# Placing the turned activations and reordering five stretches of a hand-scheduled Mamba-2 and ternary-FFN layer

## The reference

```python
# block 1: Mamba-2, then a gated MLP; rmsnorm before each
h = rmsnorm(x, ln1_w)
z, xs, B, C, dt = split(h @ w_in.T)            # 512, 128, 128, 512, 4 columns
xs, B, C = silu(causal_conv4([xs, B, C]))
dt = softplus(dt + dt_bias); a = dt * -exp(A_log)
# per chunk of 128 tokens and head: cs = cumsum(a)
Y  = ((C @ B.T) * tril(exp(cs_q - cs_k))) @ (xs * dt)
Y += exp(cs) * (C @ S);  S = exp(cs[-1]) * S + sum(exp(cs[-1] - cs) * B * xs * dt)
h = x + ((Y + D * xs) * silu(z)) @ w_out.T
m = silu(rmsnorm(h, ln2_w) @ gate_w.T) * (rmsnorm(h, ln2_w) @ up_w.T)   # 1792 wide
x = layernorm(x + h + m @ down_w.T)
# block 2: weights rounded to -1, 0, 1 times their mean magnitude (q)
x = layernorm(x + ((x @ q(w_gate).T) * (x @ q(w_up).T)) @ q(w_down).T)  # 1376 wide
```

## Time and profile before

| | before |
|---|---|
| median of 3 runs | 480.82 us (480.57 to 481.75) |
| the profiled execution | 480.79 us |
| its span, first to last instruction | 478.9 us |
| PE busy | 463.3 us (97%), 2068 matmuls and transposes |
| DVE, ACT, POOL busy | 336.8 (70%), 259.7 (54%), 233.3 (49%) |
| chain that ended last | PE 85%, DVE 5%, ACT 5%, issue 2%, POOL 2% |
| mean granted clock of TensorE | 0.999 |
| DMA | 40.81 MB, 85 GB/s |

### The profile page before, as it was taken

The page is one execution under the profiler, slowest core; times in us unless marked ns, Lnnn a source line. Parts: engine busy times, 40 slices in busy tenths (PEclk is TensorE's granted clock), DMA queues, the critical chain, the costliest instruction groups (busy, mean ns, idle before and its releaser), DMA issues.

```text
span 478.9 us, 6373 instructions
## 1 busy us (share of the span) xinstructions
PE 463.3 (97%) x2068; PEld 369.1 (77%) x2068; DVE 336.8 (70%) x579; ACT 259.7 (54%) x508; POOL 233.3 (49%) x285
## 2 busy tenths in 40 slices
PE   7999999999999969999999999999999999999995
PEld 7887777876777748888878888888887777788883
DVE  3673876655587677676799899984877665587274
ACT  4889857777656656655423344222708665658000
POOL 6474555527553468767877300026028455652022
PEclk9999999999999999999999999999999999999999
DMA  7720222021222314525313336620200010000022
GB/s 239 247 88 4 86 89 66 22 89 47 75 79 91 129 42 156 184 87 192 119 58 132 133 108 205 214 90 0 85 4 0 0 46 24 1 0 1 0 89 88
DMA packets 14432, 40.81 MB, mean 85 GB/s; under 512 B 2368, under 2 KB 2368, under 8 KB 14400
## 3 DMA queue, kind: packets, MB, share of 16 engines
q1 hardware_dynamic: 14400, 40.41, 25.2%
HBM read 38.30 MB, written 2.10 MB: 84 GB/s over the span
## 4 chain that ended last, share of the span: by engine, by line
PE 85%; DVE 5%; ACT 5%; issue 2%; POOL 2%; POOLq 0%; DVEq 0%
PE psA L1712 7%; PE psA L1714 7%; PE psA L1727 4%; PE psA L1729 4%; PE psA L1718 3%; PE psA L1720 3%; PE psB L1923 3%; PE psB L1919 3%; PE psB L1922 3%; PE psA L1700 2%; PE psA L1705 2%; PE psA L1701 2%; PE psB L2010 2%; PE psB L2011 2%; PE psB L2022 2%
## 5 line engine op out<-in xcount | busy, mean ns | idle before, releaser
L796 POOL TENSOR_SCALAR var<-mv 128x1 f32<-128x1 f32 x16 | 4.5, 280 | 108.0 <-DVE mv L1293 107.9
L858 POOL TENSOR_TENSOR beta<-wsum,beta 128x512 fp32r<-128x512 f32 x28 | 36.2, 1312 | 24.5 <-ACT beta L1060 24.5
L1182 ACT ACTIVATE c<-c 128x512 f32<-128x512 f32 x14 | 8.9, 633 | 46.9 <-DVE c L1519 46.9
L1700 PE MATMUL psA<-xT_h,win_h 128*128 128x512 f32 x80 | 32.5, 407 | 0.0
L1701 PE MATMUL psA<-xT_l,win_h 128*128 128x512 f32 x80 | 31.4, 393 | 0.0
L1419 DVE SCALAR_TENSOR_TENSOR xbc<-psA,convw_sb,xbc 128x511 f32<-128x511 f32 (+2 forms) x36 | 26.9, 747 | 4.4 <-ACT xbc L1119 3.6
L1192 ACT ACTIVATE act_hl<-act 128x512 fp32r<-128x512 f32 x28 | 16.9, 627 | 17.1 <-PE psB L1923 10.9
L1712 PE MATMUL psA<-xT_h,beta 128*128 128x512 f32 x56 | 22.4, 401 | 1.0 <-issue 0.7
L984 POOL TENSOR_TENSOR int_l<-int,int_h 128x512 fp32r<-128x512 f32 x11 | 14.3, 1298 | 18.1 <-ACT int_h L1263 18.1
L1714 PE MATMUL psA<-xT_l,beta 128*128 128x512 f32 x56 | 21.9, 391 | 0.0
L1705 PE MATMUL psA<-xT_h,win_l 128*128 128x512 f32 x80 | 21.9, 395 | 0.0
(11 more groups left out here) (336 smaller groups left out, 1591.5 us busy)
## 6 DMA issues: line engine op xcount, KB each, us to landing
raw<-in_f_gu_t SPq DMA_DIRECT2D x22, 512.0 KB, 3.4
raw<-in_w_gu_t SPq DMA_DIRECT2D x14, 512.0 KB, 3.7
raw<-in_f_dn_t SPq DMA_DIRECT2D x10, 512.0 KB, 3.4
raw<-in_w_gu_t SPq DMA_DIRECT2D x14, 256.0 KB, 2.9
raw<-in_w_dn_t SPq DMA_DIRECT2D x7, 512.0 KB, 3.9
raw<-in_w_in_t SPq DMA_DIRECT2D x5, 512.0 KB, 4.0
x<-in_hidden SPq DMA_DIRECT2D x8, 256.0 KB, 5.1
out<-x SPq DMA_DIRECT2D x8, 256.0 KB, 2.0
```

The costliest lines, as they stand in the source:

```text
L858: nc.gpsimd.tensor_tensor(beta[:, f % 2, 1, cols], wsum[:, f % 2, cols], beta[:, f % 2, 0, cols].bitcast(F32), ALU.subtract).then_inc(gb_l ...
L1700: nc.tensor.matmul(ps, sh, mh, start=i == 0, stop=False)
```

## The change

Five edits; instructions are neither added nor taken away but for one ACT table load that goes and one that comes, and one wait on POOL.

1. **Placement.** A tile of 32 floats, `to_line_of_256`, is put behind x, and `FILL` grows from 8 to 40. xT_h now begins at 17664, xT_l at 34048, raw at 50432, ident at 62720, all multiples of 256; the shared region begins at 69632, a multiple of 256 as before.
2. **Batch 1's dt.** `dt 1` moves behind the last in-projection of batch 0, `dtturn 1` and `dtlog 1` move behind `inproj 1 0`, `state 0 0` and `chunk 0 1`, next to `dtend 1`. The banks of psB are dealt out anew: outproj 0 0 now reopens the bank of cb of chunk (0,1) instead of xb's, which dtturn 1 takes.
3. **Batch 1's first chunk.** The load of the MLP weights ga 2 and its splits (ACT L1040, DVE L1348) come one in-projection later, behind turn2 0 3 instead of before decay 1 0.
4. **The scan's end** (the step s = 9). `gsplit 0 0` comes first, `trest 2` before `thigh 3`, `tlow 3` directly behind it, and the copies of p1 10 and p2 8 and `gsplit 0 1` after it.
5. **The FFN's start.** ACT does `t3high` before the copies of fb 2, fa 4 and fb 3 (a new step `fbcopy` stands for two of them), `t3low` of 2 and 3 moves from POOL to DVE, and POOL waits for all four `t4low` before the weight sums of block 3.

```diff
-FILL = 8
+FILL = 40
...
-        if j == NX + NZ - 2:
+        if j == NX + NZ - 1:
             steps.append(("dt", 1))
-        if j == NX + NZ - 1:
-            steps += [("dtturn", 1), ("dtlog", 1)]
...
         if j == 0:
-            steps.append(("dtend", 1))
+            steps += [("dtturn", 1), ("dtlog", 1), ("dtend", 1)]
...
-        if j >= NX + NZ - 4 and j < NX + NZ - 1:
-            steps.append(load("ga", j - (NX + NZ - 4)))
+        if j >= NX + NZ - 4 and j != NX + NZ - 2:
+            steps.append(load("ga", min(j - (NX + NZ - 4), 2)))
...
         elif s == NX + NZ - 1:
-            steps += before + first + after + second + [("p1", NPRE - 1)] + thigh + held + [("gsplit", 0, 0)]
+            steps += first + [("gsplit", 0, 0)] + before + after + held[:1] + thigh + held[1:] + [("tlow", *turned)]
+            steps += second + [("p1", NPRE - 1), ("gsplit", 0, 1)]
...
         x = sb("x", [P, NT, D])
+        sb("to_line_of_256", [P, 32])
...
+                if f == SUM_SLOTS:
+                    pool.wait_ge(t4_low, NC)
...
-                elif kind == "t3low":
+                elif kind == "t3low" and at[0] < 2:
...
-                elif kind == "fb":
+                elif kind == "fbcopy" or kind == "fb" and at[0] not in (2, 3):
...
+                elif kind == "t3low" and at[0] >= 2:
+                    c = at[0]
+                    v.wait_ge(t3_high, c + 1)
+                    nc.vector.tensor_tensor(xT_l[:, 0:2, chunk(NC + c)], t34[:, c, 0],
+                                            xT_h[:, 0:2, chunk(NC + c)].bitcast(F32), ALU.subtract).then_inc(t3_low, 1)
```

More of the change, by code:

```diff
@@ L167, in build_schedule @@
             steps.append(load("gb", 0))
-    steps += [("tlow", NC - 1), ("t34", NC - 1), ("trest", NC - 1), ("tlast", NC - 1), ("a22", 0), ("gsplit", 0, 1),
-              ("p2", NPRE - 2), load("gb", 1), ("a22", 1), ("p2", NPRE - 1)]
+    steps += [("t34", NC - 1), ("p2", NPRE - 2), ("trest", NC - 1), ("tlast", NC - 1), ("a22", 0), load("gb", 1),
+              ("a22", 1), ("p2", NPRE - 1)]
     assert not later and NPRE == NX + NZ + 1
@@ L252, in build_schedule @@
               ("fb", 0), ("fa", 2), ("thigh3", 2), ("fb", 1), ("turn3", 3), ("t3", 2), ("t4", 2), ("tlow3", 2),
[4 rows of a table removed]
[4 rows of a table added]
     steps += [("t4high", c) for c in range(NC)] + [("t4low", c) for c in range(NC)] + [("b22low", 3)]
-    steps += [("fopen", 1), ("fb", 4), ("f7", 0), ("wide1", ALF)]
+    steps += [("fb", 4), ("f7", 0), ("wide1", ALF)]
     assert ALF == 5 and not early
```

## The result

The changed kernel takes 478.89 us as the median of 10 runs (476.43 to 479.37), the kernel before 480.88 (480.50 to 481.75); the ratio is 0.9945, with a 95% interval of 0.9933 to 0.9957. The forecast was 476.8. The ten runs stand in two groups: four from 476.43 to 477.32, all with a mean granted clock of 0.999, and six from 478.82 to 479.37, with 0.993 to 0.995. The times of the kernel before show no such gap, but its executions are not all alike either: of the 17 beside the first experiments, eight have a mean clock of 0.999 (median 480.73) and six one of 0.992 or 0.993 (median 481.50). A clock that falls after the new wait, to which it gave a chance of 0.05, happened in six of ten runs, by their mean clocks and by the one of them that was profiled.

A forecast was written before the change was run, and what follows sets the result against it. PE was taken as the bound, with little waiting left to win. The parts, -3.5 + 3.3 - 1.2 - 1.1 - 1.5 = -4.0 against 480.79, gave 476.8 us, range 473.5 to 480.2.

The forecast's parts named there:

- the new wait: At outproj (0,0), PE waits about 3.4 us until the decay operations free the bank of cb (0,1).
- Part 1: Products moving xT: aligning xT to 256 bytes saves 5.8 ns on each of 612 matmuls, -3.5 us.
- rival (a): Products moving xT: offset does nothing, the 5.8 ns belong to SBUF part or operand row length; 480.3 us, chance 0.15.
- The formula that I quoted from the Trainium skill: Warm matmuls start N/2.4 GHz plus about 2.5 ns apart, 215.7 ns for 512 columns; placement then worth 0.
- Part 2: Batch 1's dt: the late chain delays decay (0,1) and the bank outproj (0,0) reopens, +3.3 us.
- rival (d): At outproj (0,0): PE's 3.3 us wait drops the clock to 1.2 GHz; slower, 482.8 us, chance 0.05.
- My twelve microseconds at the lower level: After the wait at outproj (0,0): twelve microseconds at 1.2 GHz, each costing 0.5 us, give 482.8 us.
- Part 4: Scan's end: the new order of splits and low parts shortens PE's waits, -1.1 us, bounds 0 and -3.8.
- The bound of -3.8: Scan's end: the most that could be gained, if DVE and POOL did not stretch each other.
- Parts 3 and 5: Batch 1's first chunk without the ga 2 split, -1.2 us; FFN's start without the wait for POOL's xT_l, -1.5 us.
- rival (c): FFN's start: DVE and POOL stretch each other and nothing is won; 478.3 us, chance 0.1.
- Rival (b): Batch 1's dt: the chain costs nothing, as DVE reaches decay before PE reaches outproj or the bank differs; 473.5 us, chance 0.2.

The follow-up runs named there:

- both at 128: The kernel before with FILL 40 and no tile behind x, so xT and the shared region both lie at 128 modulo 256: 478.29 us.
- the placement alone: The kernel before with only FILL 40 and the tile of 32 floats behind x: 478.48 us, ratio 0.9944.
- dt later still: The changed kernel with dtturn, dtlog and dtend of batch 1 moved one in-projection later, behind outproj (0,0): 475.88 us.
- dt at its old place: The changed kernel with the steps of batch 1's dt where they stood before the change: 473.27 us, ratio 0.9841.
- the dt move alone: The kernel before with only the move of batch 1's dt: six runs, 484.34 to 484.37 and 486.34 to 488.17 us, ratio 1.0101.
- the region at 128: The changed kernel with FILL at 8, so xT stays at 0 modulo 256 and the shared region goes to 128: 481.48 us.

## Why the prediction was right, and where not

| part | forecast | medians | traces, from the first transposes |
|---|---|---|---|
| 1 placement | -3.5 | -2.5 | -2.7 |
| 2 dt | +3.3 | +3.4, and 2.4 more in the second group | +3.8, and 1.2 more when the clock falls |
| 3 first chunk | -1.2 | -1.0 | -0.9 |
| 4 scan's end | -1.1 | -2.7 | -2.0 |
| 5 FFN's start | -1.5 | -1.3 | -1.7 |
| sum | -4.0 | -4.1 in the first group, -2.0 over all ten | -3.5 with the clock up, -2.4 with the fall |

**Part 1** had the right size per matmul and a wrong reason and a wrong count. 5.8 ns were (4 x 8.2 + 2 x 1.5)/6 = 6.0 by the table of starts. The reason in the text was xT's own offset; rival (a) put it on the part of SBUF. Neither is so: both at 128 is as fast as both at 0. The count was too high in the FFN. From f7 0 to the last matmul the kernel with the placement alone gained 0.36 us (100.26 against 100.62) and not 1.0. The matmuls themselves did come closer there (those that move xT_h against `w` from 237 to 231 ns, where no start is delayed), but in the first blocks PE does not run at its own pace: the first product of xT against `wsums` starts at 389.06, 395.66, 402.25 and 408.84 in the kernel before and at 387.21, 393.80, 400.38 and 406.96 with the placement alone, 6.6 us apart in both. What the pitch gave is taken back by two longer distances in each block (274 to 289 ns, at most 273 in the kernel before); what paces PE there was not tried. The formula that I quoted from the Trainium skill, which gives it for an isolated matmul, has no term for the place and so gave 0 for this part; the run of the placement alone gained 2.5.

**Part 2** had the right chain. Counted from the first transposes, which start 0.86 later than in the kernel before, ecs ended at 58.45 as I took it, log at 60.07 for 60.2, dtend at 61.40 for 61.45 and decay at 62.63 for 62.8; PE was there at 59.67 for 59.45, and waited 3.1 for 3.4. Two things were not in its sum. The chunk (0,0) that "no longer stands behind dt" did not start earlier in any useful way, because it then waited 1.2 for silu; I had costed its early start at nothing, and the hole that is left there is one of the two losses in "dt later still". And the **rival (d)** was under-priced. I put its chance at 0.05 on the ground that the clock's row never fell at the two waits before. But the longer of these stands at the start, where that row doesn't show the lower level at which PE then runs (thirty transposes 0.21 us apart at first), and the other was 1.7, so neither says what 3.3 us of idle time do. The step that failed is this one. Its price per microsecond, 0.5 us, fits the profile: a fall of some three microseconds made outproj take 4.33 us for 2.84, 1.5 more. By the last matmul 1.2 of it are left (407.5 us from outproj's start, 406.3 with dt at its old place). The two groups differ by 2.4 (medians 476.8 and 479.2). The rest fits a late start: the first transposes of the profiled run, which is of the second group, start 1.4 later than those of dt at its old place. No run of the first group was profiled, so that its runs began early is not shown. My twelve microseconds at the lower level, needed for a time above the kernel before, did not come: it was some three.

**Part 4** was under-sized: I expected the waits to be renamed with about a quarter of them gone. They went from 3.8 (1.75, 0.72, 1.33) to 1.54 (0.88, 0.66), and the run with the order undone says 2.7 by the medians, 2.0 by the traces. The bound of -3.8 held. The stretching of DVE and POOL was rightly priced (L1333 1.77 beside POOL, as before); what I missed is that the last of the three gaps would close altogether, p4 0 included.

**Parts 3 and 5** came as worked out, and rival (c), no gain at the FFN's start, is refuted: two L1638 on DVE took 1.31 beside POOL, stretched, and there was still half a microsecond to spare. Rival (b), a free dt move, is refuted by the dt move alone.

So the total of 476.8 was met by the first group alone, and by luck: two errors, +1.0 in placement and -1.6 at the scan's end by the medians (+0.8 and -0.9 by the traces), nearly cancel. The median of all ten is 2.1 above it, because six of ten runs are of the group in which the clock falls.

## What to carry to other kernels

When steps of an order are moved in a kernel that deals out PSUM banks in that order, read first which job's bank the next matmul will reopen, and what must have happened before it is free: nearly the same late chain cost 3.4 us with one bank and under 1 with another. A new wait of PE of about three microseconds has to be priced with the clock behind it, and the traces of two executions are only compared from a point behind their start. And before aligning a tile, compare its address with that of the operand that is used with it, not with zero.

## What the runs showed of the hardware

- Matmuls of 512 columns started 227 ns apart where moving and stationary operand lay alike modulo 256 bytes (both at 0, both at 128). Where they lay 128 apart, those that moved xT_h took 235 and those that moved xT_l 228; where they lay 64 apart, both took 233. That it is the stationary operand, and not another tile of the shared region, is an inference: it is the only operand of these products there. It is not the whole rule either, for the product of tT behind one of xT was slow too (231 to 233 at its start). Distances other than 0, 64 and 128 were not run.
- After PE had been idle 3.1 us in a busy stretch, the granted clock fell to the lower level for about 3 us in six of ten executions of the same program, by one trace and their mean clocks; after 4.2 us in all eleven, by one trace, their times and their mean clocks. After 3.0 us it stayed up in two traces (the dt move alone, the region at 128).
- At the program's start PE ran at half its later rate until 6.0 to 8.8 us (warm-up transposes 0.21 us apart, then 0.11), while the clock's row showed the upper level; how long this lasts moved the whole program by up to 1.4 us between executions.
- A fall need not cost much: in the profile of both at 128 the clock was 0.57 from 170 to 174 us, behind the waits at the scan's end, and from the first transposes to the last matmul it took 462.00 us, against 461.78 in the placement alone, which has no fall.
